# The last batch's closing sums and second layer norm, split into half tiles and started inside the last visit

## The reference, cut to what matters

```python
def coupling_net(h):                       # 256 -> 256 -> 128 -> 64 -> 1
    h = gelu(h @ w1 + b1); h = gelu(h @ w2 + b2); h = gelu(h @ w3 + b3)
    return sigmoid(h @ w4 + b4)

def twist(x):
    o_r, o_i, p_r, p_i = split(x, 4)       # 64 features each
    return concat([p_r, -p_i, -o_r, o_i])

gf = global_net(x1.mean(axis=1))
out = x1
for _ in range(3):
    combined = 0.7 * gf + 0.3 * coupling_net(out)
    coupling = 0.1 + adaptive_range * (combined - 0.5) * 2.0
    out = out + coupling * twist(out)
y = layernorm(x1 + out)
```

## Time and profile before

| | us |
|---|---|
| median of the runs | 1715.19 |
| lowest, highest | 1714.67, 1715.37 |
| the profiled execution's own time | 1712.26 |
| its span (first to last record) | 1710.5 |
| PE busy | 1647.6 (96%) |
| DVE busy | 1133.8 (66%) |
| ACT busy | 730.7 (43%) |
| POOL busy | 500.7 (29%) |

### The profile page before, as it was taken

The page is one execution under the profiler, slowest core; times in us unless marked ns, Lnnn a source line. Parts: engine busy times, 40 slices in busy tenths (PEclk is TensorE's granted clock), DMA queues, the critical chain, the costliest instruction groups (busy, mean ns, idle before and its releaser), DMA issues.

```text
span 1710.5 us, 49599 instructions
## 1 busy us (share of the span) xinstructions
PE 1647.6 (96%) x21456; PEld 1326.4 (78%) x21456; DVE 1133.8 (66%) x2608; ACT 730.7 (43%) x1366; POOL 500.7 (29%) x496
## 2 busy tenths in 40 slices
PE   5999999999999999999999999999999999999991
PEld 3888888885788888888588888888668888888750
DVE  6667676765476767675566767676557676766654
ACT  4434343445443434345534343435544343434554
POOL 5323232331232323233032323233213232323311
PEclk9999999999999999999999999999999999999996
DMA  4001010101001010102000101010100010100101
GB/s 165 15 2 39 2 39 2 39 14 50 2 27 26 24 30 20 33 17 73 1 15 14 39 14 39 15 39 15 62 2 14 27 27 26 27 26 15 61 15 49
DMA packets 90169, 49.54 MB, mean 29 GB/s; under 512 B 54112, under 2 KB 88800, under 8 KB 89952
## 3 DMA queue, kind: packets, MB, share of 16 engines
q1 hardware_dynamic: 89808, 46.36, 9.5%
q10 hardware_dynamic: 144, 0.00, 0.0%
HBM read 29.58 MB, written 16.78 MB: 27 GB/s over the span
## 4 chain that ended last, share of the span: by engine, by line
PE 93%; ACT 2%; DVE 2%; POOL 1%; issue 1%; DMA 0%; ACTq 0%; SPq 0%; DVEq 0%; POOLq 0%
PE bank L1244 48%; PE bank L1324 11%; PE bank L1311 8%; PE bank L1271 7%; PE bank L1503 5%; PE bank L1301 4%; PE bank L1288 4%; PE bank L1280 3%; PE bank L1228 2%; PE bank L1525 1%; ACT q_sb L752 1%; ACT x_2b L769 1%; DVE stats L880 0%; POOL pows L508 0%; DVE v_sb L1019 0%
## 5 line engine op out<-in xcount | busy, mean ns | idle before, releaser
L537 POOL TENSOR_TENSOR k_end<-k_sc,pows 128x512 f32<-128x512 f32 x128 | 135.0, 1055 | 587.5 <-DVE k_sc L929 586.6
L671 ACT ACTIVATE q_sb<-q_sb,pows 128x384 f32<-128x384 f32 (+2 forms) x384 | 167.7, 499 | 229.9 <-DVE q_sb L938 229.9
L687 ACT ACTIVATE h_sc<-h_seq,pows 128x256 f32<-128x256 f32 x128 | 65.3, 510 | 412.7 <-DVE h_seq L1103 383.6
L1103 DVE SCALAR_TENSOR_TENSOR h_seq<-h_seq,pows,bank 128x64 f32<-128x64 f32 x384 | 107.8, 281 | 201.0 <-PE bank L1288 188.3
L546 POOL TENSOR_TENSOR o_lo<-o_g,o_hi 128x512 fp32r<-128x512 f32 x128 | 165.2, 1291 | 143.9 <-ACT o_hi L693 141.1
L987 DVE COPY_PREDICATED att<-causal,bank 128x1024 f32<-128x1024 int32 x128 | 169.2, 1322 | 0.5
L693 ACT ACTIVATE o_hi<-o_g 128x512 fp32r<-128x512 f32 x128 | 80.9, 632 | 156.9 <-DVE o_g L1003 156.9
L1324 PE MATMUL bank<-wo_hi,o_hi 128*128 128x256 f32 x512 | 145.8, 285 | 1.9 <-POOL o_lo L546 1.9
L1324 PE MATMUL bank<-wo_hi,o_lo 128*128 128x256 f32 x512 | 143.0, 279 | 0.0
L1324 PE MATMUL bank<-wo_lo,o_hi 128*128 128x256 f32 x512 | 142.6, 278 | 0.0
L1311 PE MATMUL bank<-att,v_sb 128*64 128x128 f32 x2048 | 140.1, 279 | 0.6 <-DVE att L987 0.6
(11 more groups left out here) (215 smaller groups left out, 3865.4 us busy)
## 6 DMA issues: line engine op xcount, KB each, us to landing
x_in<-in_x SPq DMA_DIRECT2D x16, 512.0 KB, 3.9
x_rows<-x_nf SPq DMA_DIRECT2D x16, 512.0 KB, 2.9
x1t<-x_rows SPq DMA_DIRECT2D x32, 256.0 KB, 3.1
out_y<-x1t SPq DMA_DIRECT2D x32, 256.0 KB, 2.5
x_nf<-x_rows SPq DMA_DIRECT2D x48, 128.0 KB, 3.1
v_sb<-in_wq SPq DMA_DIRECT2D x1, 1024.0 KB, 6.3
v_sb<-in_wk SPq DMA_DIRECT2D x1, 1024.0 KB, 6.4
x1t<-in_wv SPq DMA_DIRECT2D x1, 1024.0 KB, 8.5
```

The costliest lines, as they stand in the source:

```text
L537: nc.gpsimd.tensor_tensor(k_end[:].rearrange("p (a z) (b r) -> p a (z b) r", z=2, r=BL), k_sc[:].rearrange("p (a z) (b r) -> p a (z b) r", ...
L671: last = nc.scalar.activation(q_sb[:, p % 2, d].rearrange("p (a z) n -> p a (z n)", z=2)[:, :, reach], q_sb[:, p % 2, 0].rearrange("p (a z ...
L1103: step = nc.vector.scalar_tensor_tensor(h_seq[:, c + 1, :] if c + 1 < NC else h_st[:, p, :], h_seq[:, c, :], pows[:, p, HP + 1:HP + 2], ba ...
```

## The change

Five things are done, four of them for the last batch only.

- `final_scaled` and `final_summed` take a `half`: two chunks instead of four. Each half counts its semaphore (`s_fa`, `s_fs`) by one, so every tile of every batch counts two. In batches 0 to 2 both halves are called one after the other at the place where the whole stood.
- ScalarE does the halves of tile 0 and the first half of tile 1 inside the last visit: after `layer2` of its first tile, after `layer2` of its second, and after `layer3`. The second half of tile 1 follows `layer4`. Then tile 2 is scaled, tile 0 normed, tile 3 scaled, tiles 1 and 2 normed, and of tile 3 the first two chunks.
- VectorE runs `last_sums` for a tile: sums of a half, its `bn_stats`, then the same for the other half, then the moments. It does tile 0, then the third coupling of group 1, then tiles 1, 2 and 3; the shift of a tile comes after the sums and statistics of the next one.
- GpSimd does `mix_ended` for both groups ahead of all four powers.
- The last tile's norm is shared: VectorE norms chunks 2 and 3 with one `tensor_scalar` each (`last_normed`), and SP stores these first, then ScalarE's half.

```diff
@@ -293,6 +293,7 @@
         s_st2 = sem("ln2_stats_ready")
         s_rs2 = sem("ln2_rstd_ready")
         s_fin = sem("final_rows_ready")
+        s_finv = sem("last_rows_ready_by_vector")
         s_out = [sem(f"rows_{t}_stored") for t in range(NS)]
         s_passed = sem("vector_passed")
         s_passed_pe = sem("tensor_passed")
@@ -406,8 +407,12 @@
                 put_aside(b * NS + NS - 1)
                 for t in range(NS):
                     brought_back(b, t)
-            for t in range(NS):
+            for t in range(NS - 1):
                 store(B - 1, t)
+            sp.wait_ge(s_finv, 1)
+            sp.dma_start(out_rows[B * NS - 1][:, 2:4, :], fin_rows(NS - 1, 1)).then_inc(s_out[NS - 1], 16)
+            sp.wait_ge(s_fin, B * NS + CF)
+            sp.dma_start(out_rows[B * NS - 1][:, 0:2, :], fin_rows(NS - 1, 0)).then_inc(s_out[NS - 1], 16)
             for t in range(NS):
                 sp.wait_ge(s_out[t], 16 * KT * B + C0)
 
@@ -623,13 +628,10 @@
                 mix_begun(b, 0)
                 mix_begun(b, 1)
                 mix_ended(b, 0)
-                if b + 1 == B:
-                    final_rstd(b, 0)
-                    final_rstd(b, 1)
                 mix_ended(b, 1)
                 if b + 1 == B:
-                    final_rstd(b, 2)
-                    final_rstd(b, 3)
+                    for t in range(NS):
+                        final_rstd(b, t)
 
 
         @block.scalar
@@ -712,18 +714,19 @@
                     ins = nc.scalar.activation(gf3[:], bank[7][:, 2:3], ACT.Tanh, bias=g_b3[:], scale=0.5)
                 ins.then_inc(s_ga, 1)
 
-            def final_scaled(b, t):
-
-                act.wait_ge(s_back[t], 16 * KT * (b + 1))
-                act.wait_ge(s_mix, mix_done(b, t // GT))
-                for c in range(NC):
+            def final_scaled(b, t, half):
+
+                if half == 0:
+                    act.wait_ge(s_back[t], 16 * KT * (b + 1))
+                    act.wait_ge(s_mix, mix_done(b, t // GT))
+                for c in (2 * half, 2 * half + 1):
                     last = nc.scalar.activation(summed(b, t, c), fin(t, c), ACT.Copy, scale=mix_of(t, 2, c))
                 last.then_inc(s_fa, 1)
 
-            def final_normed(b, t):
+            def final_normed(b, t, end=NC):
 
                 act.wait_ge(s_sh, b * NS + t + 1)
-                for c in range(NC):
+                for c in range(end):
                     last = nc.scalar.activation(fin(t, c), summed(b, t, c), ACT.Identity,
                                                 bias=shift[:, t, c:c + 1], scale=rstd2[:, t, c:c + 1])
                 last.then_inc(s_fin, 1)
@@ -813,7 +816,8 @@
                             if p == NP - 3 and following:
                                 x_scaled(it + 1)
                             if p == 1 and b:
-                                final_scaled(b - 1, s)
+                                final_scaled(b - 1, s, 0)
+                                final_scaled(b - 1, s, 1)
                         else:
                             o_high(p, n)
                             if following:
@@ -838,11 +842,18 @@
                 for layer in range(1, 4):
                     global_net(b, layer)
                 for v in range(VIS):
+                    ending = b + 1 == B and v + 1 == VIS
                     layer2(b, v, 0)
+                    if ending:
+                        final_scaled(b, 0, 0)
                     layer2(b, v, 1)
+                    if ending:
+                        final_scaled(b, 0, 1)
                     if v + 1 < VIS:
                         layer1(b, v + 1, 0)
                     layer3(b, v)
+                    if ending:
+                        final_scaled(b, 1, 0)
                     layer4(b, v)
                     if v + 1 < VIS:
                         layer1(b, v + 1, 1)
@@ -850,10 +861,13 @@
                     nc.scalar.activation(idle[:], gamma[:], ACT.Silu).then_inc(s_idle, 1)
                     act.wait_ge(s_idle, b + 1)
                 if b + 1 == B:
-                    for t in range(NS):
-                        final_scaled(b, t)
-                    for t in range(NS):
-                        final_normed(b, t)
+                    final_scaled(b, 1, 1)
+                    for t in range(GT, NS):
+                        for half in range(2):
+                            final_scaled(b, t, half)
+                        final_normed(b, t - GT)
+                    final_normed(b, NS - 2)
+                    final_normed(b, NS - 1, NC // 2)
 
 
         @block.vector
@@ -1004,23 +1018,40 @@
                 last.then_inc(s_og, 1)
 
             def final_stats(b, t):
-                dve.wait_ge(s_fs, b * NS + t + 1)
+                dve.wait_ge(s_fs, (b * NS + t) * 2 + 2)
                 norm_stats(lambda c: summed(b, t, c), s_st2, mv2[:, t], rstd2[:, t])
 
             def turned_back(rows, first, step):
 
                 return bass.AP(rows.tensor, rows.offset + first * DH, [list(rows.ap[0]), [step * DH, 2], [1, DH]])
 
-            def final_summed(b, t):
-
-                dve.wait_ge(s_fa, b * NS + t + 1)
-                for c in range(NC):
+            def final_summed(b, t, half):
+
+                dve.wait_ge(s_fa, (b * NS + t) * 2 + half + 1)
+                for c in (2 * half, 2 * half + 1):
                     sums = summed(b, t, c).rearrange("p (q n) -> p q n", n=DH)
                     nc.vector.scalar_tensor_tensor(sums[:, 0:4:3, :], turned_back(fin(t, c), 2, -1), mix_of(t, 3, c),
                                                    sums[:, 0:4:3, :], ALU.mult, ALU.add)
                     last = nc.vector.scalar_tensor_tensor(sums[:, 1:3, :], turned_back(fin(t, c), 3, -3), mix_of(t, 4, c),
                                                           sums[:, 1:3, :], ALU.mult, ALU.add)
                 last.then_inc(s_fs, 1)
+
+            def last_sums(b, t):
+
+                for half in range(2):
+                    final_summed(b, t, half)
+                    dve.wait_ge(s_fs, (b * NS + t) * 2 + half + 1)
+                    for c in (2 * half, 2 * half + 1):
+                        nc.vector.bn_stats(stats[:, c, :], summed(b, t, c)).then_inc(s_st, 1)
+                norm_moments(s_st2, mv2[:, t], rstd2[:, t])
+
+            def last_normed(b, t):
+
+                dve.wait_ge(s_rs2, b * NS + t + 1)
+                for c in range(NC // 2, NC):
+                    last = nc.vector.tensor_scalar(fin(t, c), summed(b, t, c), mv2[:, t, c, 0:1], rstd2[:, t, c:c + 1],
+                                                   ALU.subtract, ALU.mult)
+                last.then_inc(s_finv, 1)
 
             def rows_kept(b, t, c):
 
@@ -1121,7 +1152,8 @@
                             if p < 2:
                                 masked(n)
                             if p == 2 and b:
-                                final_summed(b - 1, s)
+                                final_summed(b - 1, s, 0)
+                                final_summed(b - 1, s, 1)
                             if p == 5 and b:
                                 final_stats(b - 1, s)
                             if p == NP - 5 and s:
@@ -1197,10 +1229,7 @@
                         third_rows(b, g, j)
                 coupling(b, visit(0, 2))
                 if b + 1 == B:
-                    for t in range(GT):
-                        final_summed(b, t)
-                        final_stats(b, t)
-                        final_shift(b, t)
+                    last_sums(b, 0)
                 if b + 1 < B:
                     for m in range(2):
                         values_kept((b + 1) * NS, m)
@@ -1210,12 +1239,11 @@
                     for m in range(2, 2 * NC):
                         values_kept((b + 1) * NS, m)
                 else:
-                    for t in range(GT, NS):
-                        final_summed(b, t)
-                    for t in range(GT, NS):
-                        final_stats(b, t)
-                    for t in range(GT, NS):
-                        final_shift(b, t)
+                    for t in range(1, NS):
+                        last_sums(b, t)
+                        final_shift(b, t - 1)
+                    final_shift(b, NS - 1)
+                    last_normed(b, NS - 1)
 
 
         @block.tensor
```

## The result

The changed kernel takes 1703.63 us (median of 4 runs, 1703.01 to 1704.23), the kernel before beside it 1714.93 us (4 runs, 1714.66 to 1715.37). The ratio is 0.9938, 95% interval 0.9926 to 0.9951: faster by 11.3 us, where 11.1 had been forecast. The profiled execution of the changed kernel took 1703.01 us with a span of 1701.3, the one of before 1712.26 and 1710.5. These two differ by only 9.25 us, and that must be cleared up before any step can be compared.

A forecast was written before the change was run, and what follows sets the result against it. The end was taken to be set by DVE's list, its late start and three waits. Stores ending 11.25 us earlier plus 0.15 contention gave -11.1 us, from 1715.19 to 1704.1 us; range 1702.8 to 1707.4.

The forecast's parts named there:

- contention: POOL's six small steps beside tile 1's sums slow three DVE instructions: 0.15 us, bounds 0 and 0.3.
- Part 1: Last visit: pairs of scalings fit ACT's holes between layers, so DVE's sums begin 5.68 us earlier, at 1674.20.
- The third hole: ACT's last gap between layers in the last visit: a scaling pair fits with 0.25 us left.
- The coupling's slack of 0.39: Group 1's third coupling on DVE: `th` is ready at 1678.19, the coupling due at 1678.58, so no wait.
- Part 2: DVE's list of tile sums, coupling and shifts runs without waits; the shift of tile 2 starts 10.67 us earlier.
- Part 3: The end: ACT norms six chunks instead of eight, 1.0 us less; 0.4 of ACT's gain is lost on the DMA queue.
- The open cost, the power beside sums: POOL's powers of tiles 0 to 2 running during DVE's sums: taken as 0, bounds 0.15 and 2.4 us.
- rival 1: POOL's power blocks DVE's sums: path 2.4 us longer, gain 8.7 us, 1706.5 us; chance 0.31.
- rival 2: ACT's holes are too small for the pairs: gain 10.1 or 8.4 us, 1705.1 or 1706.8 us; chance 0.09.
- rival 4: Path not shortened: a late half holds DVE after tile 0; end moves under 3.4 us, about 1713; chance 0.04.
- rival 3: Halves delay the attention loop in 12 tiles: 1.0 us each eats the gain, 1.5 gives 1722.1 us; chance 0.04.
- its word on the profiled execution: Whole kernel: the changed kernel's profiled execution would take 1701.2 us.

The follow-up runs named there:

- experiment 3: Changed kernel, but ScalarE norms all four chunks of the last tile and SP stores it like the others: stretch 27.31 us, median 1704.36 us.
- experiment 8: Changed kernel with tile 2's norm shared too, and tiles 1 to 3 doing all eight sums before their statistics: stretch 25.08 us, median 1701.97 us.
- experiment 1: Changed kernel, but ScalarE does all scalings of tiles 0 and 1 behind the last layer4, none in the holes: stretch 31.89 us, median 1709.33 us.
- experiment 2: Changed kernel, but group 1's third coupling follows tile 1's sums and tile 0's shift, with GpSimd's first power moved ahead: stretch 29.31 us, median 1706.01 us.
- experiment 4: Kernel before, with only final_scaled and final_summed called in halves at their old places: stretch 36.49 us, median 1711.52 us, ratio 0.9979.
- experiment 5: Changed kernel plus one unused GpSimd instruction beside tile 2's sums: multiply of 512 elements a partition, stretch 27.83 us; power of 16 elements, 26.88 us.
- experiment 7: Changed kernel and kernel before, unedited, profiled again: stretches 26.85 and 38.06 us, medians 1701.99 and 1714.93 us, ratio 0.9927.

## Why the prediction was right

The end came as forecast because it was read off one engine's list. By its own steps, in us into the stretch (the predicted path without the 0.15 for contention, which the sum adds at its end):

| step | predicted | measured |
|---|---|---|
| first sum | 1.69 | 1.59 |
| coupling of group 1 | 6.07 | 5.99 |
| tile, first sum to first sum, with shift | 4.46 | 4.46 |
| shift of tile 2 | 19.70 | 19.65 |
| ACT's last norm ends | 22.93 | 22.90 |
| stores' transfers end | 25.94 | 25.95 |
| end of the stretch against before | -11.1 | -11.10 |

The mechanism is right to 0.1 or 0.2 us at each step; that the last row agrees to 0.01 is luck. With the 0.15 the shift of tile 2, ACT's end and the transfers' end were forecast at 19.85, 23.08 and 26.09, and came 0.14 to 0.20 earlier; what follows the transfers was taken as the 0.8 us of before and is 0.94. The transfers' ends are read from slices of 0.17 and 0.26 us.

**Part 1** held, with one price off: the pair does not wait for the end of the activation (0.69) but starts 0.59 behind its start (1675.00 against 1674.41), so the first sum is 0.1 earlier. The third hole held by its margin: in experiments 3 and 8, with the same pair in it, `th` starts 5.42 and 5.41 into the stretch, before 5.41. That it is 0.28 later in the profile compared here is not the pair's doing: PE's last layer took 1.32 us, in the kernel before 1.05, at a granted clock of 0.74:

```profile
1678.74 1.32 PE L1553 MATMUL bank<-w4d,x_2b 128*128 128x2 f32 x8 [0.79 <-ACT x_2b L772]
```

```profile
1678.70:1680.10 1.40, 1.32 (x8) 1.23 (x8) 1.22 (x6) 0.78 (x3) 0.00 (x0) 0.74 0.00 0
```

The coupling's slack of 0.39 took nearly all of it: `th` ended at 1680.37, the coupling started at 1680.40.

**Part 2** held: from the first sum to the shift of tile 2 it has 18.01 us, measured are 18.06. Experiments 1 and 2 show its two large terms alone, 5.0 and 2.4 us. What the prediction did not name is what halving does by itself, although its first sum, put behind a pair, contains it: 0.8 us at each of two waits (experiment 4), which is why I missed that run.

**Part 3** held: sharing the last norm takes 1.0 from ACT, of which 0.4 reach the end (experiment 3), because the stores then stand back to back on the DMA engines. What sets the end here is ACT's norms, then 1 MB of transfer.

**Contention** was mis-sized, 0.15 predicted and 0.05 measured: only the first sum of tile 1 is longer, 0.31 to the next instead of 0.26 (1680.73 to 1681.04). POOL's small steps ran beside it.

```profile
1680.93 0.25 POOL L581 TENSOR_TENSOR mix<-cpl,mix 128x8 f32<-128x8 f32 x1
...
1685.32 1.11 POOL L557 TENSOR_TENSOR rstd<-rstd,half_neg 128x4 f32<-128x4 f32 x1 [2.08 <-DVE rstd L906]
```

**The open cost, the power beside sums, is zero**, as I took it. That was a choice between two bounds that no row had settled, with a chance of 0.31 for the other, so in part luck. The power above runs from 1685.32 to 1686.43; the sums from 1685.22 on start 0.27 and 0.26 apart. Experiment 5 widens this to 3.00 us. By the Trainium skill (SBUF — State Buffer, Who interferes with whom) the later of the two is blocked for the other's whole instruction; the trace agrees for the multiply of 512 elements (sum held 1.0 us) and disagrees for the power. The measurement decides: here an instruction's length alone does not block.

The shares of the 11.1 us, each measured alone: halves 1.5, holes 5.0, coupling ahead 2.4, shifts postponed 0.6, last norm shared 0.4, together 9.9. The rest, 1.2, belongs to no single edit: four were taken out of the changed kernel, where what remains hides part of their worth, and only halving was added to the one before. Which overlap holds how much was not measured, nor were GpSimd's new order (it moved with the coupling in experiment 2) and ACT's (tile 0 normed ahead of tile 3's scaling) taken back alone. Of the rivals, 1 falls by the sums' steps, 2 and 4 by ACT's and DVE's timelines, 3 by the loop's length in experiment 4.

What the prediction got wrong beside this is its word on the profiled execution: it put it at 1701.2, and it took 1703.01, by the clock drop near 1608. The difference of the medians is near the forecast all the same, with an interval of several us in which such drops are contained (0.9926 to 0.9951 is 8.4 to 12.7 us). In experiment 7 the same difference is 12.9 us with a stretch 11.2 shorter, so that the medians came within 0.2 of the forecast the first time is luck as well.

## What to carry to other kernels

When the end of a kernel is one engine's list of work, write the list with its start times and check for every entry when its inputs are ready; the margins, here 0.13 to 1.3 us, say which edit holds. Release a consumer as soon as its first piece is there: where the producer is faster per piece, this gains the rest of the producer's work at each wait, without moving anything. And before two profiled executions are compared, find a common event ahead of the change and measure from it; here 1.9 us lay in front of it. The same goes for medians of few runs: in experiment 4 they differ by 2.2 us more than the stretch does.

## What was not expected of the hardware

- In the changed kernel a power on GpSimd of 4 elements a partition takes 1.01 to 1.11 us, and one of 16 takes 3.00 us in experiment 5, both without any delay to sums on VectorE, while a multiply of 512 elements in 1.37 us holds one sum for 1.0.
- The kernel before had TensorE granted 1.00 near 1608 in one profiled execution and 0.50 for some 3 us in another, after gaps of about 2 us in 6 in both; between 30 and 40 us it was granted 0.83 and 0.66. The drop near 1608 makes some 1.6 of the 1.9 us between the two last visits compared here.
- A scaling on ScalarE starts 0.59 us behind the start of an activation of 128x512 that is shown as 0.69 long. The rows of before had this 0.1 already: scalings of 0.495 start 0.40 apart.
